# The product of scores and values in a gated linear attention block: fp32 in half-width tiles, or three passes over rounded parts

## The reference

```
s_t = exp(g_t) * s_{t-1} + k_t^T v_t        # per head, a 64 x 64 state
o_t = q_t s_t                               # k is already gated, g is a log decay
out = out * rsqrt(mean(out^2) + eps) * norm_w * sigmoid(h @ Wog.T)
```

## Time and profile before

| what | value |
|---|---|
| median of three executions | 3560.53 us (3555.53 to 3560.79) |
| the profiled execution: its own time, its span | 3560.53 us, 3558.8 us |
| PE busy | 3486.5 us, 98% of the span |
| PEld busy | 3243.8 us, 91% |
| DVE busy | 2274.4 us, 64% |
| ACT busy | 1520.3 us, 43% |
| POOL busy | 634.1 us, 18% |
| granted clock of PE, mean | 0.991 of full speed (2.4 GHz) |

### The profile page before, as it was taken

The page is one execution under the profiler, slowest core; times in us unless marked ns, Lnnn a source line. Parts: engine busy times, 40 slices in busy tenths (PEclk is TensorE's granted clock), DMA queues, the critical chain, the costliest instruction groups (busy, mean ns, idle before and its releaser), DMA issues. The chain is left out here.

```text
span 3558.8 us, 77638 instructions
## 1 busy us (share of the span) xinstructions
PE 3486.5 (98%) x26501; PEld 3243.8 (91%) x26501; DVE 2274.4 (64%) x5207; ACT 1520.3 (43%) x3840; POOL 634.1 (18%) x979
## 2 busy tenths in 40 slices
PE   7999999999999999999999997899999999999998
PEld 7999999999999999999999996799989999899987
DVE  4666666666666666666666666666676766767676
ACT  4545545545545545545545543333323333233332
POOL 0221121121121121121121112211111111112110
PEclk9999999999999999999999998899999999999999
DMA  4332432332332332332332334422221122212220
GB/s 150 100 84 72 106 83 72 106 83 72 106 83 72 105 83 72 105 83 72 105 84 72 105 79 125 142 71 83 81 84 71 71 83 92 73 71 77 78 93 24
DMA packets 243934, 309.03 MB, mean 87 GB/s; under 512 B 22160, under 2 KB 188064, under 8 KB 239792
## 3 DMA queue, kind: packets, MB, share of 16 engines
q1 hardware_dynamic: 243888, 308.42, 29.0%
HBM read 223.40 MB, written 84.93 MB: 87 GB/s over the span
## 5 line engine op out<-in xcount | busy, mean ns | idle before, releaser
L831 POOL TENSOR_TENSOR k_lo<-kg,k_hi 128x256 fp32r<-128x256 f32 x256 | 187.9, 734 | 1410.9 <-ACT q_hi L609 1410.9
L630 ACT ACTIVATE prob<-cum_rows,w_cur 128x128 f32<-128x128 f32 x1024 | 327.8, 391 | 257.3 <-PE psO L527 246.3
L55 PE MATMUL psJ<-h_hi,w_g_hi 128*128 128x256 f32 x1024 | 310.3, 303 | 2.6 <-DVE h_lo L696 2.6
L712 DVE TENSOR_TENSOR q_lo<-q,q_hi 64x256 fp32r<-64x256 f32 x512 | 298.5, 583 | 11.4
L55 PE MATMUL psJ<-h_hi,w_q_hi 128*128 128x256 f32 x1024 | 303.3, 296 | 0.0
L55 PE MATMUL psG<-h_hi,w_og_hi 128*128 128x256 f32 x1024 | 289.2, 282 | 7.4 <-DMA h_lo<-h_dram 7.4
L57 PE MATMUL psG<-h_hi,w_og_lo 128*128 128x256 f32 x1024 | 289.0, 282 | 0.0
L56 PE MATMUL psG<-h_lo,w_og_hi 128*128 128x256 f32 x1024 | 289.0, 282 | 0.0
L56 PE MATMUL psJ<-h_lo,w_q_hi 128*128 128x256 f32 x1024 | 284.7, 278 | 0.0
L56 PE MATMUL psJ<-h_lo,w_g_hi 128*128 128x256 f32 x1024 | 284.2, 278 | 0.0
L57 PE MATMUL psJ<-h_hi,w_g_lo 128*128 128x256 f32 x1024 | 284.0, 277 | 0.0
(11 more groups left out here) (224 smaller groups left out, 10769.8 us busy)
## 6 DMA issues: line engine op xcount, KB each, us to landing
cum_rows<-cum_dram SPq DMA_DIRECT2D x256, 256.0 KB, 5.4
grown<-cum_dram SPq DMA_DIRECT2D x512, 64.0 KB, 3.3
o_dram<-o SPq DMA_DIRECT2D x256, 128.0 KB, 1.9
o_cols<-o_dram SPq DMA_DIRECT2D x32, 1024.0 KB, 6.2
an_norm_x<-in_L_attn_x_dram SPq DMA_DIRECT2D x32, 512.0 KB, 4.2
h_dram<-h_hi SPq DMA_DIRECT2D x32, 512.0 KB, 4.0
h_dram<-h_lo SPq DMA_DIRECT2D x32, 512.0 KB, 4.7
h_hi<-h_dram SPq DMA_DIRECT2D x32, 512.0 KB, 4.0
```

The lines of the kernel that those rows point to most:

```text
L55: nc.tensor.matmul(out, w_hi, x_hi, start=first, stop=False)
L630: last = nc.scalar.activation(prob[:, 2 * c + h, :], cum_rows[:, p % 4, 2 * c + h, :], ACT.Exp, bias=w_cur[:, 0, c, 2 * p + h:2 * p + h + ...
L712: last = nc.vector.tensor_tensor(q_lo[r, :, h, :], q[r, p, :].rearrange("p (c t) -> p c t", c=NC), q_hi[r, :, h, :].bitcast(F32), ALU.subt ...
L831: nc.gpsimd.tensor_tensor(k_lo[:, :], kg[:, p, :], k_hi[:, :].bitcast(F32), ALU.subtract).then_inc(s["k_lo"], 1)
```

## The change

The product psO is no longer made in fp32. `round_v` (ACT) makes v_hi from the pair's 256 values of v, `rest_v` (POOL) the rest v_lo; a cast on ACT makes prob_hi from prob's 512 values once DVE has finished prob, and `rest_prob` (POOL) makes prob_lo. PE then runs `three_passes` for each chunk: both heads' 128 value channels as weights, both heads' probabilities as 256 moving columns. psO doubles to a whole bank, and of each chunk's result the two diagonal halves (head h's partitions with head h's columns) are used, so DVE's o is two additions over 64 partitions instead of one over 128. PE waits for v_lo and prob_lo in place of prob, and ACT's exponentials wait for prob_lo of the pair before in place of PE's product. The four new buffers take 6 KB of each partition.

```diff
@@ pe_tile
-                    pe.wait_ge(s["prob"], n + 1)
+                    pe.wait_ge(s["v_lo"], n + 1)
+                    pe.wait_ge(s["prob_lo"], n + 1)
                     hold(pe, s["o"], n)
                     for c in range(NC):
-                        for h in range(2):
-                            last = nc.tensor.matmul(psO[h * DH:(h + 1) * DH, c, :],
-                                                    v[:, c, p * P + h * DH:p * P + (h + 1) * DH],
-                                                    prob[:, 2 * c + h, :], start=True, stop=True,
-                                                    tile_position=(0, h * DH))
+                        last = three_passes(nc, psO[:, c, :, :], v_hi[:, c, :], v_lo[:, c, :],
+                                            prob_hi[:, 2 * c:2 * c + 2, :], prob_lo[:, 2 * c:2 * c + 2, :], True, True)
                     last.then_inc(s["gla"], 1)
@@ act_tile
+        def round_v(act, j, p):
+            act.wait_ge(s["by_act"], act_done(j, ("v", 5 if p > 3 else 3)))
+            hold(act, s["gla"], NP * j + p)
+            nc.scalar.copy(v_hi[:, :, :], v[:, :, p * P:(p + 1) * P]).then_inc(s["v_hi"], 1)
...
-                    hold(act, s["gla"], n)
+                    hold(act, s["prob_lo"], n)
...
+                    round_v(act, j, p)
                     if p + 1 < NP:
                         round_pair(act, j, p + 1)
                     elif proj:
                         round_pair(act, i, 0)
+                    act.wait_ge(s["prob"], n + 1)
+                    hold(act, s["gla"], n)
+                    nc.scalar.copy(prob_hi[:, :, :], prob[:, :, :]).then_inc(s["prob_hi"], 1)
@@ dve_tile
-                    nc.vector.tensor_tensor(o[:, p % 2, :, :], inter[:, :, :], psO[:, :, :], ALU.add).then_inc(s["o"], 1)
+                    for h in range(2):
+                        r = slice(h * DH, (h + 1) * DH)
+                        last = nc.vector.tensor_tensor(o[r, p % 2, :, :], inter[r, :, :], psO[r, :, h, :], ALU.add)
+                    last.then_inc(s["o"], 1)
@@ pool_tile
+        def rest_v(pool, n, p):
+            pool.wait_ge(s["v_hi"], n + 1)
+            nc.gpsimd.tensor_tensor(v_lo[:, :, :], v[:, :, p * P:(p + 1) * P], v_hi[:, :, :].bitcast(F32),
+                                    ALU.subtract).then_inc(s["v_lo"], 1)
+        def rest_prob(pool, n):
+            pool.wait_ge(s["prob_hi"], n + 1)
+            nc.gpsimd.tensor_tensor(prob_lo[:, :, :], prob[:, :, :], prob_hi[:, :, :].bitcast(F32),
+                                    ALU.subtract).then_inc(s["prob_lo"], 1)
...
                     mask_rows(pool, j, p, fill)
+                    rest_v(pool, NP * j + p, p)
                     if p + 1 < NP:
                         rest_k(pool, j, p + 1)
                     elif proj:
                         rest_k(pool, i, 0)
+                    rest_prob(pool, NP * j + p)
```

More of the change, by code:

```diff
@@ L332, in attention_pass @@
         k_lo = sb("k_lo", [P, T], F32R)
+        v_hi = sb("v_hi", [P, NC, P], F32R)
+        v_lo = sb("v_lo", [P, NC, P], F32R)
         v = sb("v", [P, NC, HID])
@@ L339, in attention_pass @@
         q_lo = sb("q_lo", [P, NC, 2, CH], F32R)
+        prob_hi = sb("prob_hi", [P, 4, CH], F32R)
+        prob_lo = sb("prob_lo", [P, 4, CH], F32R)
         cum_rows = sb("cum_rows", [P, 4, 4, CH])
@@ L358, in attention_pass @@
         psK = ps("psK", [P, 4, P])
-        psO = ps("psO", [P, NC, CH])
+        psO = ps("psO", [P, NC, 2, CH])
         psJ = [ps(f"psJ{n}", [P, 512]) for n in range(2)]
@@ L364, in attention_pass @@
         s = signals(nc, ctx, "a", "xT hT h_hi h_lo h_kept zb softin e1 l soft g_raw cum w_new n_turned n_out n_rows "
-                 "cur proj by_act k e mask kq_hi k_lo q_lo score prob kT kw inc mid state held gla inter o zero")
+                 "cur proj by_act k e mask kq_hi k_lo q_lo score prob prob_hi prob_lo v_hi v_lo kT kw inc mid state held gla inter o zero")
         s.update(norm["s"])
```

## The result

| what | before | after |
|---|---|---|
| median us (lowest to highest of four) | 3559.94 (3555.53 to 3560.79) | 3607.84 (3606.78 to 3609.07) |
| ratio, 95% interval | | 1.0136 [1.0122, 1.0148] |
| profiled execution, its span | 3560.53, 3558.8 | 3603.81, 3602.1 |
| a round (below), median of 31 | 66.75 | 67.88 |
| the last round, from psO of pair 0 to psO of pair 7 | 31.88 | 43.74 |

What follows compares the result with a forecast made beforehand. PE's own list was taken as the bound in 31 rounds, the whole chain in the last. -0.36 + 0.52 a round gives +5.0 us, the last round +7.5: 3560.5 to 3573 us, own range 3566 to 3582, overall 3556 to 3592.

Steps and rivals of the forecast that it cites:

- PE's own work: On PE from psI to psS, passes replacing fp32 products gain 0.06 us a pair, six pairs, 0.36 us a round.
- rival 4: Gaps around psO stay because they are not due to tiling: 3630 us, chance 0.05.
- Rivals 1 and 2: Passes at 0.115 with overlapping halves, 3560 to 3562, chance 0.20; h_lo no longer mattering, faster at 3549, chance 0.08.
- DVE's halves at pair 0: At a round's start o's two additions delay h_lo's fourth piece and PE's first g projection by 0.52 us a round.
- ACT and POOL: Added casts and subtractions at all pairs of the 31 rounds cost PE zero, bound 0.3 us.
- both just hidden: At pair 5 ACT's gate and POOL's prob_lo are ready before PE needs them, by 0.09 and 0.2 to 0.5 us.
- hidden, unless the addition comes on top of a lengthened q_lo: At pairs other than 0, o's longer addition fits DVE's idle time, with that exception left unpriced.
- a sign of being wrong: Listed as showing the forecast wrong: v's projection waiting for kg behind pair 4; no size given.
- Rival 3: Conversions late at pair 5, prob_lo stretched beside q_lo to 2.0 us: 3581, or 3589 with the gate late; chance 0.20.
- The pace of the projections' passes: On PE, projection passes start 0.115 us apart with nothing between them.
- The last round: With the scan alone, the longer chain adds 1.07 us a pair, 7.5 us in all, bounds 4.9 and 9.
- The loop of 5.6 over ACT and POOL: Last round's chain from exponentials through casts, k_lo, prob_lo and select: 5.6 us a pair against 4.53.

Runs made afterwards that it cites:

- e3: Kernel before with the six fp32r passes over constant buffers and o as one addition, second head's result left out: 3546.07 us, ratio 0.9966.
- e13: Kernel before with psO as two full-width fp32 products instead of four in half-width tiles, second head's result left out: 3584.68 us, ratio 1.0078.
- e1: Kernel before with o made as two additions over 64 partitions: 3587.4 us, ratio 1.0079.
- e4: Changed kernel with POOL's subtractions v_lo and prob_lo cut to one column each, every wait kept: 3576.1 us, ratio 1.0051.
- e14: Changed kernel with DVE's two halves of q_lo cut to one column each, all else kept: 3583.64 us, ratio 1.0068.
- e5: Changed kernel with o as one addition over 128 partitions, second head's result left out: 3569.8 us, ratio 1.0029.
- e12: Kernel before with o in two halves and POOL's two subtractions on constant buffers, products in fp32: 3599.22 us, ratio 1.012.
- e2: Kernel before with POOL's two added subtractions alone, on constant buffers nobody waits for: 3563.57 us, ratio 1.0013.
- e18: e15 with prob_hi and prob_lo made and waited for chunk by chunk, whole computation kept: 3554.4 us, ratio 0.9987.
- e17: Changed kernel with POOL's prob_lo made as two instructions of 256 values instead of one of 512: 3593.16 us, ratio 1.0099.
- e15: Changed kernel with DVE and ACT work reordered, last round in old form, and o of pair 0 behind prob of pair 1: 3563.33 us, ratio 1.0010.
- e10: Changed kernel with DVE's h_lo, kg and norm_x moved earlier and the last round in the old form: 3573.84 us, ratio 1.0044.

## Why the prediction was right, and where it was wrong

- **PE's own work**, -0.36 us a round: right. e3 measures -0.36, and e13 shows that the gaps were the tiles', so rival 4 falls. Rivals 1 and 2 fall with the halves, which take 0.42 each and do not overlap.
- **DVE's halves at pair 0**, +0.52: right in place and mechanism, somewhat too small. The pair grows by 0.66 in the changed kernel and by 0.75 in e1. The g projection is 0.59 longer than in e3, 0.50 of it a wait for h_lo by the profile. What the step left out is kw, queued behind the same h_lo, which costs 0.10 more; in e1 a slower pace of q's and k's passes adds another 0.10.
- **ACT and POOL**: "both just hidden", zero. For the chain that was written down, prob_hi and prob_lo at pair 5, that is right: PE waits for neither. The step that failed is the sentence of the paragraph before, "hidden, unless the addition comes on top of a lengthened q_lo". It was named, and even listed as a sign of being wrong (v's projection waiting for kg behind pair 4), and then left at zero without a price. It happens: 12.81 against 12.50 behind pair 4, 7.61 against 7.32 at pair 5 to 6, together +0.6 us a round. e4 and e14, without the subtractions or without q_lo's data, have 31 rounds that are 19.5 us shorter. That POOL's subtractions, q_lo and o's second half are all needed is what e4, e14 and e5 show: without any one of them both gaps go. e12 makes the one at pair 5 to 6 from halves and subtractions alone, where neither does it by itself (e1, e2). That ACT's emptying of g was hidden by so little is right for pair 5; e5 and e18 show it come out as a wait when something else moves. Rival 3 had the right engine pair, but put the price on prob_lo, the wrong victim: POOL's subtraction took 1.36, DVE's paid.
- **The pace of the projections' passes** was taken as fixed. From pair 7 to the next pair 0 the round is 0.13 above e3, also in e4, e5 and e14, and at pair 2 it is 0.09 above: there the passes stand 0.118 apart instead of 0.1135. What slows them wasn't found.
- **The last round**, +7.5: right in kind, 11.9 measured. The loop of 5.6 over ACT and POOL is not the one that is closed; the one through PE's passes and the one of DVE's own list (with q_lo at 2.4) are longer, 6.2 to 6.5. In e14, where q_lo has no data, and the clock is full, the forecast's loop is the one that is closed, at 5.43. The lower clock adds at most 0.3 a pair in the changed kernel, since DVE's list holds the pair at 6.2 without it. In e1 and e2, where q_lo is shorter, the same fall adds more (6.27 against 5.00 for a pair in e1).
- **Sum.** Missing in a round, by the medians: 0.14 (pair 0) + 0.6 (q_lo) + 0.09 and 0.13 (pace) = 0.96. The 31 rounds are 34.7 us longer in all where 5.0 were forecast, 29.7 missing; the last round has 4.4 more, and the rest of the kernel 3.3 less: 3573 + 29.7 + 4.4 - 3.3 = 3603.8, the time of the profiled execution. The four timed ones beside it took 3606.8 to 3609.1; thirteen executions of this kernel range from 3603.8 to 3609.4, so these 4 us are their spread.

## What to carry to other kernels

An operation added to POOL is paid by DVE: count each DVE instruction with two operands in SBUF that can start while it runs, at what is left of the POOL instruction, and then follow DVE's list to the next thing that PE waits for. Two hidden costs in one list are not hidden twice: at 98% of PE their sum has to fit in the slack, so add them before calling either zero. Where such an operation can't be avoided, cut it in pieces (e17: 3608 to 3593 us) and signal each piece (e18 against e15: a round 0.32 shorter), and look at what the extra issue time pushes back on the engine that makes the pieces.

## What the runs showed of the hardware

DVE is held, not slowed. In the trace of after, the 223 halves of q_lo that start while prob_lo runs find 1.13 us of it left and last 1.41, both on average: the rest of POOL's instruction and 0.28 more, where a half alone takes 0.42. 101 second halves that start beside the select on cum_rows, 0.63 us left, last 0.90. The 75 kw that start while v_lo runs last 0.425, as the others do, and o, mid, state and inter too are lengthened by 4 ns at most beside any POOL instruction: each of these has an operand in PSUM. The Trainium skill, "SBUF — State Buffer", section "SBUF: two separate sides", calls the shared port pair "an exclusive lock, not a bandwidth split", for a DVE operation with two SBUF inputs against a GpSimd one that reads SBUF. The trace agrees: in e14 the held operation ends 0.01 us behind POOL's, and e17 shows what follows from it. Of its own length the held one has only some 0.14 us hidden (0.42 alone, 0.28 behind the end). The prediction read its two q_lo rows as a stretch. They were a wait for an end, and the trace of before has it already. POOL, beside the second of those rows:

```profile
812.60 0.74 POOL L831 TENSOR_TENSOR k_lo<-kg,k_hi 128x256 fp32r<-128x256 f32 x1 [5.95 <-ACT q_hi L609]
813.62 0.63 POOL L825 TENSOR_SCALAR_AFFINE_SELECT cum_rows<-cum_rows 128x512 f32<-128x512 f32 x1
```

The two halves end at 813.61 and 814.53, each 0.28 us behind the end of one of these (813.33 and 814.25). From this the length of q_lo beside prob_lo could have been worked out before the run.

The hold goes the other way as well. In e17 the 286 pieces of prob_lo, 256 values each, that start while a half of q_lo runs (0.33 us of it left) last 0.93; the 64 that meet an idle DVE last 0.74.

A DVE operation over 64 partitions took as long as one over 128, 0.42 us, and the halves did not overlap. In the trace of after o's second half starts 0.43 behind the first, and the next instruction 0.455 behind the second; before, 0.33 lay between the one addition and its neighbour.

In the last round, where PE idles between short groups of passes, the granted clock fell to its half level in every version that took 37 us or more for it (0.72 in the mean after, 0.87 in e14, 0.91 in e2 with 37.1 us) and stayed at 1.00 in the others (before, e10 and e18 with 31.9, e4 with 35.3 us). The passes were then 0.21 apart instead of 0.12, and that is in the loops above.
